# Routing weights of two expert layers: spread over partitions by transfers from internal DRAM instead of selector products, with the seam between attention and the expert layers reordered

## What is computed

```python
def _L1_ffn_ref(...):                      # E, K, I, SI = 16, 4, 176, 704
    router_logits = x @ gate_w.T
    routing_probs = jax.nn.softmax(router_logits, axis=-1)
    topk_w, topk_idx = jax.lax.top_k(routing_probs, K)
    topk_w = topk_w / topk_w.sum(axis=-1, keepdims=True)
    combine = (jax.nn.one_hot(topk_idx, E) * topk_w[..., None]).sum(1)
    shared = _silu_mul(x @ shared_gate_up.T, SI) @ shared_down.T
    shared = shared * jax.nn.sigmoid(x @ shared_gate_vec.T)
    # for each expert: acc += (silu(x @ gate) * (x @ up)) @ down * combine[:, e]
```

## Time and profile before

| | us |
|---|---|
| median of 3 runs | 1059.25 (1054.9 to 1060.66) |
| the profiled execution | 1060.62 |
| its span in the profile | 1058.4 |
| PE busy | 940.8 (89%) |
| DVE, ACT, POOL busy | 729.5, 646.8, 485.2 |
| stage F, from 540 to the end | 518 of the 1058.4 |

### The profile page before, as it was taken

The page is one execution under the profiler, slowest core; times in us unless marked ns, Lnnn a source line. Parts: engine busy times, 40 slices in busy tenths (PEclk is TensorE's granted clock), DMA queues, the critical chain, the costliest instruction groups (busy, mean ns, idle before and its releaser), DMA issues.

```text
span 1058.4 us, 15635 instructions
## 1 busy us (share of the span) xinstructions
PE 940.8 (89%) x5402; PEld 768.4 (73%) x5402; DVE 729.5 (69%) x1309; ACT 646.8 (61%) x1251; POOL 485.2 (46%) x480
## 2 busy tenths in 40 slices
PE   5376677568999999999889999899999999999997
PEld 1033233346999999999878888787788888888886
DVE  6799998885777777776565765774565565666644
ACT  5857664665777777777535666545557545544553
POOL 0266551143666666765343334453343444444442
PEclk8599989687999999999889999999999999999999
DMA  9200100004000000000036000000000410000000
GB/s 314 113 0 1 60 1 0 1 1 176 2 2 1 2 1 1 2 1 2 1 134 264 1 1 1 1 2 1 1 1 1 166 58 2 1 2 1 20 1 21
DMA packets 4562, 35.92 MB, mean 34 GB/s; under 512 B 1021, under 2 KB 2149, under 8 KB 3109
## 3 DMA queue, kind: packets, MB, share of 16 engines
q1 hardware_dynamic: 4485, 34.93, 8.5%
HBM read 33.88 MB, written 1.05 MB: 33 GB/s over the span
## 4 chain that ended last, share of the span: by engine, by line
PE 47%; DVE 17%; issue 8%; POOL 8%; ACT 4%; DVEq 0%; POOLq 0%; ACTq 0%
PE psum L387 13%; PE psum L388 13%; PE psum L389 13%; POOL a_P L1890 3%; DVE a_max L1614 2%; POOL a_rk L1823 2%; POOL a_rq L1831 2%; DVE psum L1739 2%; DVE f_silu L1757 2%; PE psum L691 1%; PE psum L766 1%; PE psum L783 1%; PE psum L639 1%; ACT L1191 1%; PE psum L730 1%
## 5 line engine op out<-in xcount | busy, mean ns | idle before, releaser
L387 PE MATMUL psum<-x_norm_T_hi,f_wgu_hi 128*128 128x512 f32 x400 | 173.5, 434 | 3.8 <-DVE f_h_lo L1746 3.5
L388 PE MATMUL psum<-x_norm_T_lo,f_wgu_hi 128*128 128x512 f32 x400 | 158.9, 397 | 0.0
L389 PE MATMUL psum<-x_norm_T_hi,f_wgu_lo 128*128 128x512 f32 x400 | 158.4, 396 | 0.0
L826 ACT ACTIVATE f_h_hi<-psum 128x512 fp32r<-128x512 f32 x100 | 59.5, 595 | 107.7 <-DVE psum L1739 107.6
L387 PE MATMUL psum<-f_wd_hi,f_h_hi 128*128 128x256 f32 x400 | 121.5, 304 | 1.1 <-DVE f_h_lo L1746 0.9
L1746 DVE TENSOR_TENSOR f_h_lo<-psum,f_h_hi 128x512 fp32r<-128x512 f32 x100 | 69.0, 690 | 63.5 <-ACT f_h_hi L826 63.4
L388 PE MATMUL psum<-f_wd_lo,f_h_hi 128*128 128x256 f32 x400 | 112.7, 282 | 0.0
L389 PE MATMUL psum<-f_wd_hi,f_h_lo 128*128 128x256 f32 x400 | 112.6, 281 | 0.0
L1912 POOL TENSOR_TENSOR m_dBu<-m_du,m_Bs 128x1024 f32<-128x1024 f32 x32 | 76.1, 2381 | 69.2 <-DVE m_du L1333 24.8
L1836 POOL TENSOR_TENSOR f_wgu_lo<-f_w,f_wgu_hi 128x512 fp32r<-128x512 f32 x44 | 56.7, 1288 | 97.4 <-ACT f_wgu_hi L826 97.4
L1836 POOL TENSOR_TENSOR f_wgu_lo<-f_wb,f_wgu_hi 128x512 fp32r<-128x512 f32 x36 | 46.6, 1293 | 116.1 <-ACT f_wgu_hi L826 116.1
(11 more groups left out here) (329 smaller groups left out, 2716.6 us busy)
## 6 DMA issues: line engine op xcount, KB each, us to landing
f_wb<-in_f1b SPq DMA_DIRECT2D x1, 6912.0 KB, 20.1
f_w<-in_f3w SPq DMA_DIRECT2D x1, 5376.0 KB, 17.8
f_wa<-in_f1a SPq DMA_DIRECT2D x1, 3840.0 KB, 14.2
w_raw<-in_w0raw SPq DMA_DIRECT2D x1, 3072.0 KB, 18.5
f_w<-in_f2w SPq DMA_DIRECT2D x1, 3072.0 KB, 25.3
a_wo<-in_wo SPq DMA_DIRECT2D x2, 1024.0 KB, 13.1
a_wq<-in_wq SPq DMA_DIRECT2D x1, 2048.0 KB, 26.4
x_res<-in_x SPq DMA_DIRECT2D x1, 1024.0 KB, 8.9
```

The source lines that it names most:

```text
L387: mm(out, wh, xh, start=start, stop=False, **kw)
L388: mm(out, wh, xl, start=False, stop=False, **kw)
L389: return mm(out, wl, xh, start=False, stop=stop, **kw)
L826: return A(out_, in_, ACT.Copy)
```

## The change

Selector products go. The transposed weights are kept in fp32 (`weights_T`, one buffer `cmbT`), SP stores them to an internal DRAM tensor (`store_rows`, 17 or 9 rows of 2 KB, four times in all), and ACT issues, for each weighted tile, one transfer for each expert that owns some of its 128 partitions (`routing_rows`; `pieces` cuts a tile where the owner changes), each reading one row of 2 KB again and again into those partitions. They go into three buffers `cw` per layer, two tiles ahead. `weighted` reads `cw` in place of bank 6, and the product of silu and up goes to PSUM for all tiles.

```diff
+    def pieces(l, j):
+        cuts = [p for p in range(P) if p == 0 or owner(l, j * P + p) != owner(l, j * P + p - 1)] + [P]
+        return [(a, b, owner(l, j * P + a)) for a, b in zip(cuts, cuts[1:])]
+    CW_AT = [max(g - 2, cmb_at[FT[g][0], FT[g][1]] + 1 if FT[g][:2] != (1, 0) else -1) if WEIGHTED[g] else None for g in range(FN)]
 @block.sync
+        def store_rows(l, h):
+            n = (E1 if l == 1 else E3) + 1
+            sp.wait_ge(S("b7_free"), bank7.index(("cmbT", l, h)) + 1)
+            sp.dma_start(routed_rows[l, h][0:n, :], cmbT[0:n, :]).then_inc(S("cw_stored"), 16)
+    (1, 0) ahead of the loads of step 3, (1, 1) ahead of those of step 4, (3, 0) and (3, 1) behind all loads
 @block.tensor, ffns
-                mm(ps[:, 6, :], sel[l][:, j, :], cmbT[h][:, :], start=True, stop=True).then_inc(S("f_cw"), 1)
...
-                if 1 <= g <= FN:
-                    combine(g - 1)
-                if 1 <= g < FN:
+                if 2 <= g < FN:
                     gate_up(g)
 @block.scalar
+        def routing_rows(g):
+            l, h, q, j = FT[g]
+            r = ROUTED[g]
+            act.wait_ge(S("cw_stored"), 16 * (routed_index[l, h] + 1))
+            if r >= 3:
+                act.wait_ge(S("f_h"), r - 2)
+            for a, b, row in pieces(l, j):
+                nc.scalar.dma_start(cw[l][r % 3][a:b, :], routed_rows[l, h][row, :].partition_broadcast(b - a)).then_inc(S(f"cw_loaded{r % 3}"), 16)
+        (ffns, after silu(g) and side(2 * g))
+                for f in range(max(g, 3), min(g + 3, FN)):
+                    if CW_AT[f] == g:
+                        routing_rows(f)
 @block.vector, weighted
-                dve.wait_ge(S("f_cw"), ROUTED[g] + 1)
-                V.tensor_tensor(ps[:, 2 + 2 * (g % 2), :], sg[g % 2][:, :], ps[:, 6, :], ALU.mult).then_inc(S("f_h"), 1)
+                dve.wait_ge(S(f"cw_loaded{ROUTED[g] % 3}"), CW_LOADED[g])
+                V.tensor_tensor(gate, gate, cw[FT[g][0]][ROUTED[g] % 3][:, :], ALU.mult).then_inc(S("f_h"), 1)
```

The five operations of `router_split` go. At the seam the order changes:

```diff
 PE, attn1
-                    router_logits(1, 0).then_inc(S("b7_put"), 1)      (all four token tiles, before step 30)
+                    router_logits(1, 0, 0)                            (two of them there,
+                if i == HEADS2 - 2:
+                    router_logits(1, 0, 2).then_inc(S("b7_put"), 1)    two after the scores of step 30)
+                if i == HEADS2:
+                    pe.wait_ge(S("a_exp"), HEADS2)
+                    gate_up(0)
+                    pe.wait_ge(S("a_kT"), HEADS2)
+                    pe.wait_ge(S("f_cmb"), 1)
+                    weights_T(1, 0).then_inc(S("b7_put"), 1)
...
+                if i == HEADS2 + 1:
+                    gate_up(1)                                         (ahead of the last output product)
 ACT, attn1
+                if i == HEADS2 - 1:
+                    act.wait_ge(S("a_s"), HEADS2 - 1)
+                    gu_hi(0)
+                if i == HEADS2:
+                    A(scratch[:, 20:21], epsc[:, :], ACT.Silu)         (the table load, moved up)
+                    act.wait_ge(S("a_s"), HEADS2)
+                    gu_hi(1)
+                    silu(0)
...
                     d_hi(0)
+                    for g in range(3):
+                        routing_rows(g)                                (ahead of ac_hi(31))
 DVE, attn1
+                if i == HEADS2 - 1:
+                    router_top(1, 0)                                   (ahead of ac_lo(29))
-            router_split(1, 0)
             ac_lo(HEADS2 - 2)
...
+            V.tensor_copy(cmbT[0:E1 + 1, :], ps[0:E1 + 1, 7, :]).then_inc(S("b7_free"), 1)
+            silu_up(0)
             probs_lo(HEADS2 - 1)
             ac_lo(HEADS2 - 1)
```

The last product of probabilities and context goes to bank 6 (`AC_BANK`), and POOL does `gu_lo(0)` in step 31. In the list of side work the butterflies become eight pieces of one block each, logits are made in two halves at two places, and several places move:

```diff
-    put_norm(1, 1, 3, 5, 6, 7, 9, 10, 13, 15, 18)
+    put_norm(1, 1, 3, 5, 6, 7, 8, 9, 10, 13, 15)
     put_map(12, 2)
-    put_attention(2, 0, P1 + 2, P1 + 4, P1 + 8, P1 + 12, P1 + 16, P1 + 20, P1 + 24)
+    put_attention(2, 0, P1 + 2, P1 + 4, P1 + 8, P1 + 13, P1 + 15, P1 + 18, P1 + 22)
-    for n, p in enumerate((44, 48, 52, P1)):
+    for n, p in enumerate((44, 48, 52, P1, P1 + 6, P1 + 10, P1 + 14, P1 + 19)):
         put(p, "butterfly", n)
-    put_norm(2, 0, P1 + 30, P1 + 32, P1 + 35, P1 + 37)
+    put_norm(2, 0, P1 + 30, P1 + 33, P1 + 35, P1 + 37)
     put_map(P1 + 12, 3)
-    put_norm(3, 0, P3 + 9, P3 + 10, P3 + 12, P3 + 13, P3 + 14, P3 + 15, P4 + 1, P4 + 3, P4 + 4)
+    put_norm(3, 0, P3 + 9, P3 + 10, P3 + 12, P3 + 13, P3 + 14, P3 + 15, P4, P4 + 1, P4 + 2)
-    put_norm(3, 1, P4 + 17, P4 + 19, P4 + 20, P4 + 22, P4 + 24, P4 + 26, P5, P5 + 2, P5 + 4)
+    put_norm(3, 1, P4 + 17, P4 + 19, P4 + 20, P4 + 22, P4 + 23, P4 + 24, P4 + 26, P5, P5 + 1)
```

More of the change, by code:

```diff
@@ L107, in flamingo_kernel @@
     at["B0"] = at["B1"] = at["B3"] = at["B"]
-    sel = {1: place("B1", "sel1", [96, NJ[1], P], bf16)}
+    cw = {1: [place("B1", f"f1_cw{i}", [P, HALF]) for i in range(3)]}
+    at["B1"] += 1024
     fr = {1: place("B1", "f1_router", [P, KC, 32])}
@@ L113, in flamingo_kernel @@
     f3w = place("B3", "f3_w", [P, NJ[3], WJ])
-    sel[3] = place("B3", "sel3", [96, NJ[3], P], bf16)
+    cw[3] = [place("B3", f"f3_cw{i}", [P, HALF]) for i in range(3)]
     fr[3] = place("B3", "f3_router", [P, KC, 32])
@@ L194, in flamingo_kernel @@
     at["W2"] = max(at["W2"], at["qsq"])
-    cmbT = [place("W2", f"r_combine_T{i}", [96, HALF], bf16) for i in range(2)]
+    cmbT = place("W2", "r_weights_T", [24, HALF])
+    routed_rows = {(l, h): nc.dram_tensor(f"r_rows{l}{h}", (24, HALF), f32, kind="Internal").ap() for l in (1, 3) for h in range(2)}
     xTl1 = place("W2", "x_norm_T1_lo", [P, KC, HALF], f32r)
@@ L297, in put_norm @@
         for p, what in zip(places, (("stats", (f"F{l}", h)), ("normalise", (f"F{l}", h)), ("xT", l, h, 0), ("xT", l, h, 1),
[L298 removed]
+                                    ("logits_half", l, h), ("logits", l, h), ("route", l, h), ("route_top", l, h), ("cmbT", l, h))):
             put(p, *what)
@@ L362, in _ @@
                 else:
+                    if step == 3:
+                        store_rows(1, 0)
                     begin(sp, step)
@@ L578, in gate_up, with router_logits @@
                 last.then_inc(S("f_up" if b else "f_gate"), 1)
-        def router_logits(l, h):
+        def router_logits(l, h, t0):
             xh, xl = xTp[h]
             pe.wait_ge(S("r_w"), 1 if l == 1 else 2)
-            for t in range(TH):
+            for t in (t0, t0 + 1):
                 sl = slice(t * P, (t + 1) * P)
@@ L704, in attn1 @@
                     pe.wait_ge(S("xT_ready"), 2)
+                if i == HEADS2 + 1:
+                    gate_up(1)
                 if i >= 2:
@@ L732, in side @@
                     _, l, h = w
-                    use_bank7(w)
-                    last = router_logits(l, h)
+                    last = router_logits(l, h, 2)
+                elif kind == "logits_half":
+                    _, l, h = w
+                    use_bank7(("logits", l, h))
+                    router_logits(l, h, 0)
+                    continue
                 elif kind == "cmbT":
@@ L1046, in d_hi, with silu @@
             copy(wdh[g % 3][:, :], raw_w(l, j)[:, GU:WJ]).then_inc(S("f_wdh"), 1)
+        def routing_rows(g):
[6 more added lines that the diff above has]
+                nc.scalar.dma_start(cw[l][r % 3][a:b, :], routed_rows[l, h][row, :].partition_broadcast(b - a)).then_inc(S(f"cw_loaded{r % 3}"), 16)
+        def silu(g):
+            act.wait_ge(S("f_gate"), g + 1)
+            if g >= 2:
+                act.wait_ge(S("f_m"), g - 1)
+            A(sg[g % 2][:, :], ps[:, 2 + 2 * (g % 2), :], ACT.Silu).then_inc(S("f_sg"), 1)
         def router_exp(l, h):
-            rl, rp, rw, rc = ((first_routing if (l, h) == (1, 0) else routing)[n] for n in (1, 2, 5, 6))
+            rl, rp, rw, rc = ((first_routing if (l, h) == (1, 0) else routing)[n] for n in (0, 1, 4, 5))
             e = E1 if l == 1 else E3
@@ L1620, in attn1 @@
                     query_norms(i + 1)
+                    if i == HEADS2 - 2:
+                        dve.wait_ge(S("b7_put"), bank7.index(("logits", 1, 0)) + 1)
+                        take_logits(1, 0)
                     keys_lo(i + 1)
```

145 lines of the change are left out of this document (58 added, 87 removed).

## The result

Four executions of the changed kernel took 1044.5 us in the median (1043.2 to 1049.6), the kernel before beside them 1059.95 (1054.9 to 1060.9): ratio 0.9874, 95% interval 0.9837 to 0.9911. The direction was right, the size was not: 15.5 us gained of 33 forecast, 2.5 us above the range. A second set of runs of the same kernel gave 1046.2 (ratio 0.9898 [0.9854, 0.9942]).

A forecast was written before the change was run, and what follows sets the result against it. PE, busy 89% of the span, was taken to bound the kernel. Terms 18.2 + 6.8 + 3.4 + 5.4 + 3.0 - 4 = 32.8 us off 1060.6 gave 1027.8, by the median 1026.5 us, range 1018 to 1042.

The forecast's parts named there:

- F: Added transfers in stage F: 2 us charged for ACT's issues at map pairs, 2 us for the loads at its start.
- D: Butterflies in eight pieces: halved pieces delay DVE about 1.7 instead of 3.3 us; 5.4 of 5.9 us gained.
- A: Stage F, 80 selector products removed from PE at 0.23 us each: 18.2 us gained.
- R4: Rival: little changes, as combine products stood in a shadow or PE waits instead; about 1056 us, chance 0.05.
- B: Seam from attention to stage F: gate_up(0) fills PE's stop, 2.5 us of waits instead of 9.3; 6.8 us gained.
- C: Logits in halves, 12 narrow products in a row: two half-clock stretches go, 3.4 us gained.
- E: Attention steps of layer 2 moved off the places of map steps: PE's waits there go, 3.0 us gained.
- R2: Rival: ACT's serial issues set the pace, PE waits 0.2 us per weighted tile; 1040.5 us, chance 0.12.
- R1: Rival: small transfers take turns with big loads' rows, 8 us more than charged at tiles 4, 5; 1035, chance 0.15.
- R3: Rival: rows land too late all along, slower from 8.8 us landing, 1106 us at 10 us; chance 0.05.

The follow-up runs named there:

- v5: Changed kernel with the logits of (1,0) and (1,1) whole again, 24 narrow products in one row: 1048.9 us, one execution.
- v7: Changed kernel with the four map weights issued ahead of the two big loads and those cut into two-tile pieces: 1034.49 us, ratio 0.9807 to the kernel before.
- v6: Changed kernel with the butterflies in four pieces of double size again, as before the change: 1047.3 us, one execution.
- v3: Changed kernel without the stores and row transfers, multiplier set to one (part of the computation missing): 1044.5 us, ratio 0.9888 to the kernel before.
- v10: Changed kernel plus both load edits, butterflies on POOL, and routing-weight transposes of (3,1) one tile later: 1024.19 us, ratio 0.9706 to the kernel before.
- v2: Changed kernel with the four 64 KB map weights issued ahead of the two big loads: 1045.33 us, ratio 0.9888 to the kernel before.
- v1: Changed kernel with the two big loads cut into pieces of two tiles, rows of 6 KB: 1049.85 us, ratio 0.9926 to the kernel before.

## Why the prediction was wrong, point by point

Three steps failed, the largest first: the load window, charged with 2 us in F, cost 11; halved butterflies in D gave 1.9 us instead of 5.4; and of A's products some 4 us were not to be had, since they stood ahead of waits.

**A, selector products, right in price, wrong in reach.** 0.25 us each where no wait stands (0.23 forecast). But in tiles 7 to 22 the fifteen products gave 1.5 instead of 3.75 us (from tile 8 on, where executions repeat, 1.8 instead of 3.5), and in 22 to 35 thirteen gave at most 1.3 of 3.25: there PE waits for DVE (for `f_w` of the mix at tiles 14 and 16, for the lo rows behind butterflies), and a product taken out in front of a wait only lengthens it. That is R4's mechanism, in a third of the tiles. I had summed 80 equal prices.

**B, the seam, right at its place.** From the end of head 30's context products to `gate_up(2)` 13.2 us, "about 13" forecast, 20.3 before. 2.3 us of the 7.1 were given back one head earlier: from the start of head 29's products to the end of head 30's 9.7 us became 12.0. That leaves 4.8 where 6.8 was forecast, inside the bounds of 3 and 9. PE's timeline of the changed kernel there (the last row is `gate_up(0)`):

```profile
516.82 0.39 PE L418 MATMUL psum<-a_PT_hi,a_ctx_tok_hi 128*128 128x256 f32 x1 [1.75 <-DVE a_PT_lo L1624]
...
523.37 1.29 PE L732 MATMUL psum<-ident_f,a_P 128*128 128x128 f32 x8 [1.91 <-DVE a_AC_lo L1619]
...
528.80 0.39 PE L418 MATMUL psum<-x_norm_T_hi,f_wgu_hi 128*128 128x512 f32 x1
```

DVE was late at 522.56 behind the routing's small operations, one of which, on 64 elements with both inputs in SBUF, took 1.43 us. The same operation took 0.23 us in the kernel before, at 526.91. POOL's rows say why: an operation of POOL ran from 518.24 to 520.13, and DVE's ended at 520.21.

```profile
518.78 1.43 DVE L1566 TENSOR_TENSOR r_weights_first<-r_probs_first,r_replaced_first 128x64 f32<-128x64 f32 x1
```

```profile
518.24 1.89 POOL L1931 TENSOR_TENSOR a_P<-a_P,a_row_inv 128x1024 f32<-128x1024 f32 x1 [4.39 <-DVE a_row_inv L1684]
```

The cast of 1.78 us that the earlier trace rows shows ended at 530.52, and POOL's operation beside it, in the kernel before, ended at 530.47:

```profile
528.58 1.89 POOL L1890 TENSOR_TENSOR a_P<-a_P,a_row_inv 128x1024 f32<-128x1024 f32 x1 [6.01 <-DVE a_row_inv L1645]
```

So I had put down to the casts what by these rows was mostly waiting for POOL. Neither was tried by itself.

**C, half right** and hidden: what was gained in clock behind tile 4's logits was lost in the wait of tile 5 (tiles 4 and 5 together 14.15 and 14.57 us in the two traces of the changed kernel, 14.64 in v5). With that wait gone, in v7, they take 11.20 at full clock, 13.06 before. In attention no run shows a gain.

**D, the step that failed by its reason.** "Halved pieces delay DVE by about 1.7 instead of 3.3 us." The rows gave 3.2 us for a piece of 512 elements (1.47, 1.25, 0.53), and I halved it. A good part of that is not work but waiting for POOL, which doesn't halve: the first small piece took 1.47 + 0.84 + 0.29 = 2.6, the one that POOL left alone 0.42 + 0.43 + 0.29 = 1.14. And the added pieces, on tiles of the second half of layer 1, I had put at nothing: tiles 31 to 35 cost 2.4 more than in v6. Worth 1.9 instead of 5.4, and against the kernel before nothing. The 5.9 us that I saw to gain were PE's idle time and its clock; the butterflies cost 9.8 even in eight pieces.

**E, right**: tiles 36 to 41 gain 4.7 us, 1.25 of them the five selectors: 3.5 for 3.0. It was read from the traces and not tried apart.

**F, the step that failed by its size.** ACT's issues cost next to nothing (v3). The section of the Trainium skill that I had cited for 50 ns (DMA: Bandwidth & Descriptors, Anatomy of one DMA) describes transfers that GpSimd issues; an issue of ACT showed as 345 ns in the median. The view of the tile `f_cw`:

```profile
L1082 ACTq DMA_DIRECT2D f_cw<-r_rows x122: 308/345/614, 535.9 to 1028.0; - x122
```

A pair of tiles with a map step (from tile 49 on) fell from 5.09 + 4.43 to 4.84 + 4.19, by two products exactly, so R2 falls. The window I had charged with 2 us, and it cost 11 (v7 gives 10.9 back). R1 was the mechanism of one half: rows that take turns with 54 KB rows. I gave it 0.15 and 8 us, though the earlier trace rows had all that it needs. The other half I missed: the earlier trace rows shows the last map weight issued at 549.63; in that trace it landed 24.7 us later, at 574.3, and PE's map step stands behind `gate_up(6)` of 572.63, some 1 us later. A seam that runs ahead of the end of attention, on which the issue hangs, overruns it. R3 falls (4.19 in every plain tile).

**At tile 86** the moved transposes of (3,1) wait 1.84 us for DVE, a price that I had not looked for; 1.04 came back at tile 88.

The sum for the profiled pair, from tile 2 to 99: 4.0 us gained, 496.7 to 492.8; the rest of the 11.0 lies ahead of it, where executions scatter, and in the last tile. With the window as forecast it would have been some 15; with butterflies that cost nothing 10 more. v10 has 471.6.

## What to carry to other kernels

Price a removed instruction per place, not per kernel: ahead of a wait it is worth nothing. When a change shortens the path to a stage, list the loads of that stage with issue, landing and first use, and put the small and early ones first and cut long rows; and where one repair of such a window moves nothing, try both before calling it bandwidth. Work on DVE whose operands all lie in SBUF, beside a busy POOL, is better given to POOL where POOL has idle time.

The best kernel here is v10: 1024.2 us, 2.9% below the kernel before the change by its ratio, where the change alone has 1.3%.

## What the hardware showed that was not expected

- DVE against POOL: an operation of DVE with both inputs in SBUF that begins under one of POOL's ends 0.28 us (256 elements) or 0.55 us (512) behind it; alone it takes 0.42 or 0.68. The excess was 1.05 us at most for both sizes, and none for those with an operand in PSUM.
- Two queues on the same engines: a transfer of up to 128 rows of 2 KB landed after 1.6 to 4.2 us outside the load window, and after up to 19.6 beside rows of 54 KB (up to 25.4 in v2).
- SP's issues are no fixed price either: in v1 they took 0.33 to 0.71 us up to the tenth big piece, 1.7 to 3.5 for the last three, and 4.2 and 2.1 for the two small ones behind them; SP's timeline of v1:

```profile
544.52 4.56 SPq L401 DMA_DIRECT2D f_wb<-in_f1b  x9
...
550.13 8.37 SPq L401 DMA_DIRECT2D f_w<-in_f2w  x4
558.54 4.18 SPq L399 DMA_DIRECT2D am_wq<-in_am3q  x1
562.76 2.10 SPq L399 DMA_DIRECT2D am_wk<-in_am3k  x1
```
